# Moving four projection units behind the last turns of the feed-forward stages, and the last residual behind four rotary turns

## The chip, the cores and the metric

The kernel is one program on one core of a Trainium2 chip. The metric is the device time of an execution in microseconds; a measurement is the median of several runs. All matrix work is on TensorE (PE), element work on VectorE (DVE), ScalarE (ACT) and GpSimd (POOL), and SyncE (SP) issues the DMAs.

## The reference

Two pre-layernorm decoder layers on x (8 sequences of 112 tokens, width 512; 896 tokens, so seven tiles of 128). Each layer is self-attention, cross-attention and a feed-forward block:

```
x = x + L0_attn(layernorm(x));  x = x + L0_xattn(layernorm(x), ctx);  x = x + L0_ffn(layernorm(x))
x = x + L1_attn(layernorm(x));  x = x + L1_xattn(layernorm(x), ctx);  x = x + L1_ffn(layernorm(x))

L0_ffn: h = bitlinear(x, w_fc); h = gelu(h); return bitlinear(h, w_proj)
bitlinear(x, w): layer-norm x, round-trip it through absmax quantization, multiply by ternarized w
L1_attn: q = x @ Wq.T (16 heads of 128); k, v = x @ Wk.T, x @ Wv.T (4 heads)
         q, k = rope(q), rope(k); softmax(q k / sqrt(128), causal window) v; @ Wo.T
```

The change lies where L0_ffn ends and the query and key projections of L1_attn begin.

## The kernel before

The program is written as one queue of instructions for each engine, stage by stage, with semaphores between them. An engine works through its queue in the order written, so the order below is the order of the work. Products are made with operands split in two parts: XT[0] holds the rounded transposed activations and XT[1] the remainder; a weight piece lies in HL in the same two parts (round_w on ACT makes the first, rest_w on POOL the second). `mm3` (L250 to L252) issues three matmuls for one product.

**The feed-forward stages** (`pe_ffn`, `act_ffn`, `dve_ffn`, `pool_ffn`) run over st = 0 to 8. In stage st tile f = st goes through the first product (L1309, PSUM banks 0 to 3) and GELU, tile p = st - 2 is turned (four `turn`s of four transposes each, L255, banks 4 to 6), split in two parts by ACT and DVE (L1330, L1363) and multiplied by the second weights (`product`, L1294, 32 matmuls into bank 7), and the finished tile r = st - 3 is turned for the next layer. In stages 7 and 8 there is no first product any more, only p = 5, 6 and r = 4, 5.

`norm` on DVE follows the product of tile t: it adds to x (L1387), takes statistics (L1390, L1392), waits for ACT's root (L1358) and writes the normalised rows xn (L1398). `ln_turn` on PE (L322) waits for xn and transposes it into bank 7. `ln_hi` on ACT (L327) copies it rounded to XT[0], and `ln_lo` on DVE (L331) subtracts to get XT[1]. `product` of tile t waits for the ln_lo of tile t - 1, since they share bank 7.

**The projection** (`pe_proj1`, `dve_proj1`, `pool_proj1`) has 40 units, made by `unit1`. A unit is 12 matmuls, 128 columns of weight against half of the tokens (448), into bank u % 8. Units 0 to 3 are two weight pieces (q1, 0 and 1) against the first half of the tokens, which lie in tiles 0 to 3; unit 4 is the first that reads the second half, so it waits for ln_lo of tile 6. `unit1` waits for the multiplications of unit u - 8 before it writes its bank again. For each unit DVE makes three multiplications for the rotary embedding (L1498 to L1500), and POOL adds their results (L1511). DVE's unit u waits for POOL's unit u - 2, since there are two buffers rt. The V products follow on PE behind unit 39, then the attention. When POOL has summed the unit that ends a weight piece (the first time unit 5), it makes the second part of the piece three further on.

PE's order before, in stage 7: turn (5,0), turn (5,1), unit 0, ln_turn of tile 4, turn (5,2), turn (5,3), product of tile 5. In stage 8: the same with tile 6, unit 1 and ln_turn of tile 5. `pe_proj1` then has unit 2, ln_turn of tile 6, unit 3, the wait for ln_lo of tile 6, unit 4 and on. On DVE ln_lo of tile 6 is the first instruction of `dve_proj1`, ahead of the multiplications of unit 0.

Of the kernel before, what the change touches and what calls it, by code (L numbers as in the profile page):

```python
# [15 lines left out]
P, NT = 128, NB * S // 128  # L16
# [57 lines left out]
def build(nc, g):  # L74
# [8 lines left out]
    with ExitStack() as ctx:  # L83
# [136 lines left out]
        def done(sem, *point, by=1):  # L220
            count[sem] = count.get(sem, 0) + by
            assert live[0] or (sem, point) not in value, (sem, point)
            value[sem, point] = count[sem]
            return handle(sem), by
# [4 lines left out]
        def upon(sem, *point):  # L229
            return handle(sem), value[sem, point] if live[0] else 1  # L230
# [18 lines left out]
        def mm3(e, out, lh, ll, rh, rl, start, stop):  # L249
            e.matmul(out, lh, rh, start=start, stop=False)  # L250
            e.matmul(out, lh, rl, start=False, stop=False)  # L251
            return e.matmul(out, ll, rh, start=False, stop=stop)  # L252

        def tr(e, out, in_, n):
            return e.transpose(out, in_, C("ident", n)[:, 0:n])  # L255
# [6 lines left out]
        def k4(bank):  # L262
            return PS[:, bank, :].rearrange("p (k s) -> p k s", k=4)

        def XTt(hl, t):
            return XT[:, hl, :, t * P:(t + 1) * P]
# [8 lines left out]
        def slot(k):  # L275
            return HL[cut_no[k] % NHL]
# [22 lines left out]
        def has_w(e, k):  # L299
            e.wait_ge(*upon("pool_w", k))  # L300
            return slot(k)
# [19 lines left out]
        def ln_turn(e, tag, t, src, bank):  # L321
            e.wait_ge(*upon("dve_ln", tag, t, "xn"))  # L322
            turn4(e, src, bank).then_inc(*done("pe_ln", tag, t))
# [5 lines left out]
        def ln_lo(e, tag, t, bank):  # L329
            e.wait_ge(*upon("act_ln", tag, t, "hi"))  # L330
            e.tensor_tensor(XTt(1, t), k4(bank), XTt(0, t).bitcast(F), A.subtract).then_inc(*done("dve_ln", tag, t, "lo"))  # L331
# [761 lines left out]
        def w_rows(which, m, c):  # L1093
            return which[m][0][:, c, :] if m == 0 or c < 14 else which[m][1][:, c - 14, :]
# [87 lines left out]
        def quant_turn(e, t):  # L1182
            e.wait_ge(*upon("dve_fq", "y", t))
            if t < 4:
                e.wait_ge(*(upon("dve_fq", "lo", t - 1) if t else upon("dve_ox", "v", OX - 1)))
            turn4(e, xz[t % 4], q_bank(t)).then_inc(*done("pe_fq", t))
# [76 lines left out]
        def at_step(st):  # L1263
            return (st if st < NT else None, st - 2 if st >= 2 else None, st - 3 if st >= 3 else None)

        def g_of(t):
            return Gb[t % 3][:, :, :].rearrange("p a c -> p (a c)")


        def late_quant(st, n):  # L1270
            return {(0, 1): 4, (0, 3): 5, (1, 1): 6}.get((st, n))

        def pe_ffn(e):
            def turn(t, c4):
                if c4 == 0:
                    e.wait_ge(*upon("pool_f", "y", t))
                if c4 == 3:
                    e.wait_ge(*upon("dve_f", "lo", t, 0))
                elif t == 0:
                    e.wait_ge(*upon("dve_fq", "lo", 4 + c4))  # L1280
                else:
                    e.wait_ge(*upon("dve_f", "lo", t - 1, 3 if c4 == 0 else c4))
                for kc in range(4):
                    o = (c4 * 4 + kc) * 128
                    last = tr(e, PS[:, 4 + c4 % 3, kc * P:(kc + 1) * P], g_of(t)[:, o:o + 128], P)
                last.then_inc(*done("pe_f", "turn", t, c4))

            def product(t, c4):
                e.wait_ge(*upon("dve_f", "lo", t, c4))
                if c4 == 0:  # L1290
                    e.wait_ge(*(upon("dve_ln", "lnf", t - 1, "lo") if t else upon("act_sign", 1, 6)))
                for kc in range(4):
                    for hl in range(2):
                        last = e.matmul(PS[:, 7, :], YT[c4][:, hl, kc, :], w_rows(ter, 1, c4 * 4 + kc),  # L1294
                                        start=c4 == 0 and kc == 0 and hl == 0, stop=c4 == 3 and kc == 3 and hl == 1)
                last.then_inc(*done("pe_f", "pj", t, c4))

            e.wait_ge(*upon("act_sign", 0, 7))
            for st in range(NT + 2):
                f, p, r = at_step(st)  # L1300
                for n in range(4):
                    if f is not None:
                        if n == 0:
                            e.wait_ge(*upon("dve_fq", "lo", f))
                        if st:
                            e.wait_ge(*upon("act_f", "g", f - 1, n))
                        for kc in range(4):
                            for hl in range(2):
                                last = e.matmul(PS[:, n, :], XT[:, hl, kc, f * P:(f + 1) * P], w_rows(ter, 0, 4 * kc + n),  # L1309
                                                start=kc == 0 and hl == 0, stop=kc == 3 and hl == 1)  # L1310
                        last.then_inc(*done("pe_f", "fc", f, n))
                    if late_quant(st, n):
                        quant_turn(e, late_quant(st, n))
                    if p is not None and n != 2:
                        turn(p, min(n, 2))
                    if n == 2 and st >= NT:
                        unit1(e, st - NT)
                    if r is not None and n == 2:
                        ln_turn(e, "lnf", r, xn[r % 2], 7)
                if p is not None:  # L1320
                    turn(p, 3)
                    for c4 in range(4):
                        product(p, c4)

# [98 lines left out]
        def pool_ffn(e):  # L1423
            for t in range(NT):
# [8 lines left out]
        units1 = ([("q1", i, e_, h) for h in (0, 1) for i in range(2) for e_ in range(2)]  # L1433
                  + [(kind, i, e_, h) for kind, a, n in (("q1", 2, 8), ("k1", 0, 2)) for i in range(a, n)
                     for e_ in range(2) for h in range(2)])
# [11 lines left out]
        def unit1(e, u):  # L1447
            kind, i, e_, half = units1[u]
            k = piece[kind, i][0]
            if e_ == 0 and (u < 4 or u > 7 and half == 0):  # L1450
                has_w(e, k)
            if u == 0:
                e.wait_ge(*upon("act_f", "g", NT - 1, 3))
                e.wait_ge(*upon("dve_ln", "lnf", 3, "lo"))
            if u > 7:
                e.wait_ge(*upon("dve_p1", u - 8))
            project(e, slot(k), 128 * e_, half, u % 8).then_inc(*done("pe_p1", u))
            if u in ended1:
                freed[k] = "pe_p1", u

        def pe_proj1(e):
            for u in range(2, len(units1)):
                if u == 3:
                    ln_turn(e, "lnf", NT - 1, xn[0], 7)
                if u == 4:
                    e.wait_ge(*upon("dve_ln", "lnf", NT - 1, "lo"))
                unit1(e, u)
            for vh in range(2):
                k = piece["v1", vh][0]
                w = has_w(e, k)  # L1470
                for b in range(NB):
                    e.wait_ge(*(upon("act_v1", 0, b) if vh else upon("dve_p1", 32 + b)))
                    for kc in range(4):
                        o = kc * 256
                        last = mm3(e, PS[0:S, b, 0:256], XT[:, 0, kc, b * S:(b + 1) * S], XT[:, 1, kc, b * S:(b + 1) * S],
                                   w[:, 0, o:o + 256], w[:, 1, o:o + 256], kc == 0, kc == 3)
                    last.then_inc(*done("pe_v1", vh, b))
                freed[k] = "pe_v1", vh, 7
# [9 lines left out]
                round_w(e, piece["o1", 1 + vh][0])  # L1488

        def dve_proj1(e):  # L1490
            ln_lo(e, "lnf", NT - 1, 7)
            for u in range(len(units1)):
                u0, u1 = [rt[u % 2][:, j, :].rearrange("p (b s) -> p b s", b=4) for j in range(2)]
                bank = u % 8
                if u > 1:
                    e.wait_ge(*upon("pool_p1", u - 2))
                e.wait_ge(*upon("pe_p1", u))
                e.tensor_tensor(u0, psv(bank), b4(C("cos1")), A.mult)  # L1498
                e.tensor_tensor(u1[0:64], psv(bank, 64, 128), b4(C("sin1")[64:128]), A.mult)
                e.tensor_tensor(u1[64:128], psv(bank, 0, 64), b4(C("sin1")[0:64]), A.mult).then_inc(*done("dve_p1", u))  # L1500
# [976 lines left out]
```

## Time and profile before

| | |
|---|---|
| median of 3 runs | 1756.52 us (1754.92 to 1761.06) |
| the profiled execution, its own time | 1756.52 us |
| its span, first to last instruction | 1754.7 us |
| PE busy | 94% of the span |
| DVE busy | 58% |
| ACT busy | 41% |
| POOL busy | 28% |
| mean granted TensorE clock | 0.977 of full speed |

The profile is one execution seen by the hardware profiler. Each row of a timeline gives an instruction or a run of like ones: start and length in us, engine, line of the kernel, output and inputs, count, and in brackets how long the engine sat idle before it and what released it. Matmuls overlap in the array, so a matmul's length is longer than the distance to the next start; starts are the better ruler. PEclk is the granted clock as a share of full speed.

### The profile page before, as it was taken

The numbers are of one execution on the slowest core, as the hardware profiler recorded it, in microseconds if no ns is written. First come the engines' busy times: TensorE is split into PE (matmuls) and PEld (weight loads), VectorE is DVE, ScalarE is ACT, GpSimd is POOL, SyncE is SP. The second block draws the span as 40 slices with busy tenths as digits, with TensorE's granted clock in tenths as the row PEclk, the third lists the DMA queues.
The fourth block names the chain that finished last, engine by engine and source line by source line (L and its number), as shares of the span: only waits on it lengthen the run. The fifth ranks groups of instructions, "written<-read, shape, count | busy, mean of one in ns | idle before, by whom it ended". The sixth has DMA issues, their size and how long they took to land.

```text
span 1754.7 us, 24103 instructions
## 1 busy us (share of the span) xinstructions
PE 1642.1 (94%) x9652; PEld 1360.8 (78%) x9652; DVE 1020.4 (58%) x1719; ACT 726.4 (41%) x1220; POOL 497.6 (28%) x324
## 2 busy tenths in 40 slices
PE   5998999989899999989999989999788999989999
PEld 4997666868678888767889987777567788877887
DVE  5554564264557675577758757354756545554545
ACT  2111555222367775647521146222435334343332
POOL 2971443340100001321117734111512322212221
PEclk9998999989999999999999999999889999999999
DMA  3210002213321103410001110110001111111111
GB/s 133 72 49 14 2 1 80 83 49 114 105 89 52 34 1 138 153 49 1 1 1 61 48 37 1 47 36 30 19 1 54 37 55 49 61 43 36 55 61 42
DMA packets 28018, 87.48 MB, mean 50 GB/s; under 512 B 4090, under 2 KB 4090, under 8 KB 27655
## 3 DMA queue, kind: packets, MB, share of 16 engines
q1 hardware_dynamic: 27908, 85.94, 14.8%
q8 instruction: 77, 1.26, 0.3%
q14 instruction: 33, 0.27, 0.1%
HBM read 84.10 MB, written 1.84 MB: 49 GB/s over the span
## 4 chain that ended last, share of the span: by engine, by line
PE 80%; DVE 8%; ACT 7%; issue 2%; DMA 1%; POOL 1%; SPq 0%; ACTq 0%; DVEq 0%
PE PS L250 17%; PE PS L252 16%; PE PS L251 16%; PE PS L255 6%; PE PS L957 4%; PE PS L975 4%; PE PS L1294 3%; PE PS L845 3%; PE PS L1309 2%; PE PS L518 2%; ACT Sk L586 1%; PE PS L1543 1%; ACT PT L578 1%; PE PS L1531 1%; DMA stg<-in_wst 1%
## 5 line engine op out<-in xcount | busy, mean ns | idle before, releaser
L296 POOL TENSOR_TENSOR HL<-stg,HL 128x1024 fp32r<-128x1024 f32 (+2 forms) x109 | 237.9, 2185 | 866.2 <-ACT HL L291 866.2
L250 PE MATMUL PS<-XT,HL 128*128 128x448 f32 x608 | 224.8, 370 | 8.3 <-DVE XT L331 6.1
L251 PE MATMUL PS<-XT,HL 128*128 128x448 f32 x608 | 223.1, 367 | 0.0
L252 PE MATMUL PS<-XT,HL 128*128 128x448 f32 x608 | 223.1, 367 | 0.0
L291 ACT ACTIVATE HL<-stg 128x1024 fp32r<-128x1024 f32 (+2 forms) x109 | 102.2, 943 | 261.5 <-PE PS L252 240.8
L250 PE MATMUL PS<-HL,XT 128*128 128x512 f32 (+1 forms) x380 | 139.0, 366 | 8.9 <-DVE XT L678 7.4
L251 PE MATMUL PS<-HL,XT 128*128 128x512 f32 (+1 forms) x380 | 136.0, 358 | 0.0
L252 PE MATMUL PS<-HL,XT 128*128 128x512 f32 (+1 forms) x380 | 135.9, 358 | 0.0
L250 PEld LDWEIGHTS PS<-XT,HL 128*128 128x128 f32 x608 | 115.0, 189 | 19.7 <-DVE XT L331 5.3
L251 PEld LDWEIGHTS PS<-XT,HL 128*128 128x128 f32 x608 | 115.0, 189 | 9.2
L252 PEld LDWEIGHTS PS<-XT,HL 128*128 128x128 f32 x608 | 114.9, 189 | 9.1
L2112 DVE SCALAR_TENSOR_TENSOR Hh<-PS,sml,Hh 128x448 fp32r<-128x448 f32 x64 | 43.2, 682 | 106.7 <-ACT Hh L2006 106.5
L678 DVE TENSOR_TENSOR XT<-QO,XT 128x896 fp32r<-128x896 f32 x32 | 45.0, 1432 | 98.5 <-ACT XT L672 98.5
L957 PE MATMUL PS<-kvT,QO 128*112 128x375 f32 x256 | 92.5, 484 | 2.7 <-ACT Sx L1002 2.0
L250 PE MATMUL PS<-HL,Ph 128*128 128x512 f32 x224 | 91.2, 407 | 3.7 <-DVE ACC L2135 1.8
L1021 DVE TENSOR_REDUCE nm<-PS 112x2 f32<-112x750 f32 x64 | 60.1, 939 | 51.6 <-PE PS L957 51.6
L250 PEld LDWEIGHTS PS<-HL,XT 128*128 128x128 f32 (+1 forms) x380 | 70.9, 187 | 22.9 <-issue 7.0
L252 PE MATMUL PS<-HL,Ph 128*128 128x512 f32 x224 | 88.2, 394 | 0.0
L251 PE MATMUL PS<-HL,Ph 128*128 128x512 f32 x224 | 88.0, 393 | 0.0
L975 PE MATMUL PS<-PX,kvr 125*128 125x224 f32 x384 | 85.3, 359 | 0.0
L2006 ACT ACTIVATE Hh<-PS,sml 128x448 fp32r<-128x448 f32 x64 | 40.4, 634 | 103.0 <-PE PS L252 103.0
L651 POOL TENSOR_TENSOR Sk<-Sk,rc 112x896 f32<-112x896 f32 x32 | 53.3, 1682 | 100.2 <-DVE rc L633 100.2
(285 smaller groups left out, 3705.4 us busy)
## 6 DMA issues: line engine op xcount, KB each, us to landing
stg<-in_wst SPq DMA_DIRECT2D x85, 512.0 KB, 3.4
stg<-in_wst SPq DMA_DIRECT2D x16, 352.0 KB, 3.2
stg<-in_wst SPq DMA_DIRECT2D x16, 320.0 KB, 3.7
wsum<-in_wfc SPq DMA_DIRECT2D x8, 512.0 KB, 4.9
wsum<-in_wpj SPq DMA_DIRECT2D x8, 512.0 KB, 3.6
raw<-in_wfc SPq DMA_DIRECT2D x8, 512.0 KB, 7.6
stg<-in_wst SPq DMA_DIRECT2D x16, 256.0 KB, 2.6
raw<-in_wpj SPq DMA_DIRECT2D x7, 512.0 KB, 7.2
```

What stands on the lines that cost most here:

```text
L250: e.matmul(out, lh, rh, start=start, stop=False)
L251: e.matmul(out, lh, rl, start=False, stop=False)
L252: return e.matmul(out, ll, rh, start=False, stop=stop)
L255: return e.transpose(out, in_, C("ident", n)[:, 0:n])
L291: e.activation(slot(k)[:, 0, 0:n], stg[k % NSTG][:, 0:n], ACT.Copy).then_inc(*done("act_w", k))
L296: e.tensor_tensor(slot(k)[:, 1, 0:n], stg[k % NSTG][:, 0:n], slot(k)[:, 0, 0:n].bitcast(F), A.subtract).then_inc(*done("pool_w", k))
L651: e.tensor_tensor(p, p, b8(rc[:, k, :]), A.mult).then_inc(*done("pool_a0", "p", u))
L845: last = e.matmul(out, Mhl[i][:, a, kc, :], XT[:, c, kc, hs], start=kc == 0 and j == 0, stop=kc == 3 and j == 2)
L957: last = e.matmul(PS[0:S, bank + e_, 0:L], QO[:, 1 + st // 4, 2 * (st % 4) + e_, :], kvT[:, b, :], start=True, stop=True)
L975: last = e.matmul(PS[:, 6 + u % 2, 0:2 * S], kvr[:, c, u // 4 % 8, :], PX[u % 2][:, :, c, :], start=c == 0, stop=c == 2)
L1021: e.tensor_reduce(nm[:, st % 4, :], PS[0:S, bank:bank + 2, 0:L], AX.X, A.max, negate=True).then_inc(*done("dve_x", "nm", st))
L1294: last = e.matmul(PS[:, 7, :], YT[c4][:, hl, kc, :], w_rows(ter, 1, c4 * 4 + kc), start=c4 == 0 and kc == 0 and hl == 0, stop=c4 == 3 and ...
```

## The change

Units 0 and 1 go from the middle of stages 7 and 8 to behind the last turn of stage 7, ahead of the product of tile 5. Units 2 and 3 go from `pe_proj1` to the same place in stage 8, ahead of the product of tile 6. `pe_proj1` begins with ln_turn of tile 6 and the wait for its ln_lo, then unit 4. On DVE, ln_lo of tile 6 goes from ahead of the multiplications of unit 0 to ahead of those of unit 4, behind those of units 0 to 3. No arithmetic, buffer, DMA or semaphore is added or removed.

```diff
                     if p is not None and n != 2:
                         turn(p, min(n, 2))
-                    if n == 2 and st >= NT:
-                        unit1(e, st - NT)
                     if r is not None and n == 2:
                         ln_turn(e, "lnf", r, xn[r % 2], 7)
                 if p is not None:
                     turn(p, 3)
+                    if st >= NT:
+                        for u in range(2 * (st - NT), 2 * (st - NT) + 2):
+                            unit1(e, u)
                     for c4 in range(4):
                         product(p, c4)
...
         def pe_proj1(e):
-            for u in range(2, len(units1)):
-                if u == 3:
+            for u in range(4, len(units1)):
+                if u == 4:
                     ln_turn(e, "lnf", NT - 1, xn[0], 7)
-                if u == 4:
                     e.wait_ge(*upon("dve_ln", "lnf", NT - 1, "lo"))
                 unit1(e, u)
...
         def dve_proj1(e):
-            ln_lo(e, "lnf", NT - 1, 7)
             for u in range(len(units1)):
+                if u == 4:
+                    ln_lo(e, "lnf", NT - 1, 7)
```

## Rows read from the trace of the kernel before

**Rows 1.** The page: busy time by engine, and the chain that ended last.

```profile
PE 1642.1 (94%) x9652; PEld 1360.8 (78%) x9652; DVE 1020.4 (58%) x1719; ACT 726.4 (41%) x1220; POOL 497.6 (28%) x324
...
PE 80%; DVE 8%; ACT 7%; issue 2%; DMA 1%; POOL 1%; SPq 0%; ACTq 0%; DVEq 0%
```

**Rows 2.** Busy time by stretch, PE alone: us, busy (instructions), granted clock, DMA share, GB/s.

```profile
885.00:917.00 32.00, 30.13 (x159) 1.00 0.00 1
916.67:1026.90 110.23, 110.23 (x625) 1.00 0.16 53
```

**Rows 3.** Timeline of PE in stage 7: start, length in us; idle before, and releaser.

```profile
885.01 1.04 PE L255 MATMUL PS<-cst,Gb 128*128 128x128 f32 x8
885.80 0.45 PE L250 MATMUL PS<-XT,HL 128*128 128x448 f32 x1
...
888.32 0.60 PE L255 MATMUL PS<-cst,xn 128*128 128x128 f32 x4
888.75 1.04 PE L255 MATMUL PS<-cst,Gb 128*128 128x128 f32 x8
890.42 0.94 PE L1294 MATMUL PS<-ter,YT 128*128 128x512 f32 x3 [0.63 <-DVE XT L331]
```

**Rows 4.** Timeline of PE from stage 8's product on, and the first V product.

```profile
903.21 6.60 PE L1294 MATMUL PS<-ter,YT 128*128 128x512 f32 x28 [0.63 <-DVE XT L331]
909.64 1.07 PE L1294 MATMUL PS<-ter1e,YT 128*128 128x512 f32 x4
...
913.75 0.66 PE L255 MATMUL PS<-cst,xn 128*128 128x128 f32 x4 [0.61 <-DVE xn L1398]
...
916.67 0.36 PE L250 MATMUL PS<-XT,HL 128*128 128x448 f32 x1
...
1004.22 0.28 PE L250 MATMUL PS<-HL,XT 128*112 128x256 f32 x1
```

**Rows 5.** Timeline of DVE, stages 7 and 8 and behind them.

```profile
887.61 0.55 DVE L1398 TENSOR_SCALAR xn<-x,mvl,rsl 128x512 f32<-128x512 f32 x1
888.07 1.28 DVE L1363 TENSOR_TENSOR YT<-PS,YT 128x512 fp32r<-128x512 f32 x2
889.58 0.69 DVE L331 TENSOR_TENSOR XT<-PS,XT 128x512 fp32r<-128x512 f32 x1 [0.23 <-ACT XT L327]
...
913.15 0.55 DVE L1398 TENSOR_SCALAR xn<-x,mvl,rsl 128x512 f32<-128x512 f32 x1
915.07 0.69 DVE L331 TENSOR_TENSOR XT<-PS,XT 128x512 fp32r<-128x512 f32 x1 [1.38 <-ACT XT L327]
915.68 0.61 DVE L1498 TENSOR_TENSOR rt<-PS,cst 128x448 f32<-128x448 f32 x1
...
917.60 0.62 DVE L1498 TENSOR_TENSOR rt<-PS,cst 128x448 f32<-128x448 f32 x1
```

**Rows 6.** Timeline of POOL: unit 0's sum, and the first weight piece behind the change.

```profile
917.65 1.16 POOL L1511 TENSOR_TENSOR QO<-rt 128x448 f32<-128x448 f32 x1 [30.70 <-DVE rt L1500]
...
928.39 2.40 POOL L296 TENSOR_TENSOR HL<-stg,HL 128x1024 fp32r<-128x1024 f32 x1
```

**Rows 7.** Waits of PE from 916 to 1040 us: total, times, longest.

```profile
PE PS L255 <- POOL Sb L1572: 1.2, 1, 1.2
```

**Rows 8.** Windows around holes of PE: columns as in rows 2.

```profile
742.00:748.00 6.00, 3.85 (x16) 1.00 0.25 81
766.00:778.00 12.00, 9.70 (x41) 0.86 0.00 0
804.00:814.00 10.00, 7.96 (x32) 0.83 0.01 2
1159.00:1172.00 13.00, 8.95 (x32) 0.87 0.11 40
481.00:492.00 11.00, 7.24 (x24) 0.69 0.55 194
372.00:400.00 28.00, 20.73 (x97) 0.70 0.32 102
```

## The prediction

> **What bounds the kernel now.** I read the page first: TensorE (PE) is busy for 94% of the span, and the chain that ended last lies on it for 80% [rows 1]. So a change costs or gains what it does to the holes in PE's stream. Next, busy time by stretch. Around the moved units, from 885 us to the start of unit 4 (916.67), PE is busy for 30.13 of 32.00 us: it has 1.87 us of holes there, which is all that a new order could win. From unit 4 to the end of the V products PE is busy for 110.23 of 110.23 us [rows 2]: whatever delays unit 4 delays the whole rest. The reader is to see that the first number bounds the gain, and that the second takes away any later repayment.
>
> Then the timelines of PE and VectorE (DVE). Three things fill the time of a norm. In stage 7, two turns start at 885.01, unit 0 runs from 885.80 to the turn of the normalised rows at 888.32, and those rows are finished by DVE at 887.61 + 0.55 = 888.16 [rows 3, 5]. The unit therefore hides the norm, to within 0.2 us. Stage 8 is the same 12.79 us later (product at 903.21 against 890.42), with unit 1 [rows 3, 4]. Behind the last product, unit 2 hides most of the third norm (0.61 us left), and unit 3 hides the copy and the subtraction L331 [rows 4, 5].
>
> **The change part by part.**
>
> *Units 0 and 1 leave the hole of the norm.* Unit 0 no longer stands between the turns and ln_turn of tile 4, and unit 1 is no longer in stage 8. In stage 7, PE ends the two turns at 885.01 + 1.04 = 886.05, and has nothing to do until the rows at 888.16; the first transpose after such a wait comes 0.05 us later (913.15 + 0.55 = 913.70, then 913.75), so at 888.21: a new hole of 2.16 us [rows 3 to 5]. ln_turn starts only 0.11 us earlier than before. Its four transposes take 0.43 us to the next start and eight turns 0.79 us [rows 3], so the units can start at 888.21 + 0.43 + 0.79 = 889.43. The last turn needs the first split of tile 5, which DVE makes first in the pair at 888.07 (1.28 us for two), so by about 888.7; no wait [rows 5].
>
> *Two units per stage behind the turns.* A unit that follows transposes takes 888.32 - 885.80 = 2.52 us, one that follows a unit 2.43 us: units 4 to 39, 36 of them, take from 916.67 to the first V product at 1004.22 [rows 3, 4]. 889.43 + 2.52 + 2.43 = 894.38 for the start of the product, against 890.42: **+3.96 us**. The hole of 0.63 us ahead of the product goes, since splits and L331 are done by then; it is in this difference already. Stage 8 is the same pattern with units 2 and 3: again +3.96 us, together **+7.92 us**. Of that 4.86 us is work brought forward from behind the last product.
>
> *Behind the last product nothing is left to hide the norm of tile 6.* The last product ends at 909.64 + 1.07 = 910.71 in the trace of before, and the rows are ready at 913.70 [rows 4, 5]. All 2.99 us of it is idle now.
>
> *DVE turns four units before it does L331.* This is the costly edit. The DVE queue is written out in order. Before, L331 of tile 6 (dve_proj1's ln_lo) ran at 915.07 and the rotary multiplications of unit 0 came behind it at 915.68. Now the multiplications of units 0 to 3 stand first. None of them waits: their products are long there, and GpSimd's sum, which a unit's multiplications wait for two units later, takes 1.16 us [rows 6] of a unit's 1.92 us. Their period is 917.60 - 915.68 = 1.92 us, so four take 7.69 us [rows 5]. They start as the norm ends, 0.08 us before its modelled end as the split at 888.07 does against 888.16, so at 913.62. L331 starts at 921.31 and ends at 922.00. PE starts 0.15 us behind such an end (889.58 + 0.69 = 890.27 against 890.42 in the stage before; I take this lag for unit 4 too). Unit 4 starts at 922.15, that is 11.44 us behind the last product. Queued behind L331 on DVE are the multiplications of unit 4 on, which need PE's unit 4 anyway; PE's whole queue waits for L331. ScalarE's copy of tile 6 is ready long before, as it was at 915.07.
>
> Before, unit 4 started 916.67 - 910.71 = 5.96 us behind the product, with two units in that time [rows 4]. So this end costs 11.44 - 5.96 = **+5.48 us**. Sum on PE at an unchanged clock: 7.92 + 5.48 = **+13.4 us**.
>
> *What it doesn't cost.* The bytes, weights and matmuls are the same, and no DMA is moved in its queue. The first new weight piece is finished by GpSimd at 928.39 + 2.40, behind its sum of unit 5 [rows 6], for unit 12. GpSimd is four units ahead in the new order when unit 4 starts, so it is earlier against PE than now, when PE doesn't wait. That cover is PE's own 19 us from unit 4 to unit 12 (eight units of 2.43 us); without it a late piece costs what it is late by. The head start of DVE and GpSimd is worth nothing: in the stretch to 1040 PE's longest wait is for GpSimd in the attention, 1.2 us [rows 7], and in the 110 us of units and V products there is none [rows 2].
>
> *TensorE's clock.* A hole can cost more than its length. The windows around holes of before show it [rows 8], each around one long hole but for the last row: idle time is the window less PE's busy time, and time lost to the clock is window x (1 - PEclk), as the granted clock has two levels, 1.2 and 2.4 GHz. Around 804 to 814 (2.04 us idle) 10 x 0.17 = 1.7 us is lost; at 766 (2.30 us idle) 12 x 0.14 = 1.7; at 1159 (4.05 idle) 13 x 0.13 = 1.7; at 481 (3.76 idle) 11 x 0.31 = 3.4. But 742 to 748 (2.15 idle) lost nothing. The new holes are 2.16 us in stages 7 and 8, and behind the last product 2.99 us plus, behind one turn (913.75 + 0.66 = 914.41), 922.15 - 914.41 = 7.74 us, more than any of these. For the last I take one fall, **1.7 us** (ends: 0 and 3.4, taken from the rows at 1159 and 481; nearer 1159, since units of long matmuls follow it). For each short hole I take 0.6 as the chance of a fall (two of the three rows nearest in length fell). One fall of the two is likelier (0.48) than both (0.36) or none (0.16): **1.7 us**, ends 0 and 3.4.
>
> The Trainium skill (TensorE: Matmul & The Clock Gate, HAM oscillation) warns only of holes longer than these two short ones. By it the short ones lose nothing, and the sum would be 15.1 us in place of 16.8. The hole in the window from 804, as short, did lose 1.7 us in this trace, so I go by the row and keep the rule as a rival.
>
> **Sum.** 13.4 + 1.7 + 1.7 = +16.8 us. The profiled execution took 1756.52 us for a span of 1754.7, and is itself the median of the three runs (1754.92 to 1761.06). 1756.5 + 16.8 = **1773.3 us**, slower by 0.96%. No change is anything within 0.3%, 5.3 us.
>
> **The rivals.**
> - *Both short holes lower the clock:* 13.4 + 1.7 + 3.4 = 18.5, 1775.0 us. The rows at 766 and 804 speak for it, 742 against.
> - *Only the long hole does:* 15.1, 1771.6 us. Beside it: this is what the page of the Trainium skill named above would lead to. The row at 804 speaks against.
> - *The clock stays up everywhere:* 13.4, 1769.9 us. Against it: both windows with over 3.5 us idle lost some, and 7.7 us is far more.
> - *The clock costs more:* behind the long hole 3.4 or, as at 372 to 400 [rows 8], where PE had hole after hole, 28 x 0.30 = 8.4 us. With one short hole that is 18.5 to 23.5 us, 1775 to 1780. Against it: unit 4 on is a stream without holes, and 372 to 400 was none.
> - *Not slower:* the three holes of before (0.63, 0.63, 0.61 us) go and no new one comes, which gives 1756.5 - 1.9 = 1754.6 us. The place is L331 of tile 6: it decides if DVE has done the four units' multiplications before PE is through its last product. But DVE's norm of tile 6 needs that product and stands ahead of them in the queue. A gain beyond 0.3% isn't to be had at all, as the stretch has only 1.87 us of holes [rows 2].
>
> **How the numbers follow.** The three ways the short holes can go, 0.48, 0.36 and 0.16, share the 0.83 that the other cases leave: forecast 0.40; both short holes 0.30; only the long one 0.13; clock unchanged 0.05; clock costs more 0.09; not slower 0.03. The range takes 1769.9 (less 1.6, the lowest of the runs before against their median) and 1775.0 plus 3, into the dearer case and the runs' upward spread: 1768.3 to 1778. All but the last case are over 0.3% slower: slower 0.96, same 0.03, faster 0.01.
>
> **What would show it.** In stages 7 and 8: a hole of 2.2 us ahead of ln_turn that waits for xn L1398, then two units in a row, and no wait for L331 at the product; product starts 16.75 us apart, or up to 1.7 more. Behind the last product: about 3.0 us idle, one turn, then 7.7 us idle, ended by L331, which starts right behind twelve multiplications of DVE. From there to the attention a PE as full as now, with a stretch at half the clock first. The prediction is wrong if L331 comes ahead of the multiplications, if PE waits for weights in unit 12, or if PE falls behind DVE's head start and wins something back in the attention.

## The result and the profile after

The changed kernel is slower: ratio 1.0069 to the kernel before, 95% interval 1.0044 to 1.0095, medians 1771.4 us (1762.67 to 1773.69) and 1756.45 us, six runs each. By the ratio that is +12.2 us, by the medians +15.0. A second comparison, in experiment 5, gave 1.0088 (1.0063 to 1.0113). The profiled execution took 1766.8 us with a span of 1765.0 us, against 1756.52 and 1754.7; it lies 4.6 us below the changed kernel's median.

The timeline of PE of the changed kernel, stage 7 to unit 4, and the first V product, answers to [rows 3] and [rows 4]:

```profile
885.23 1.04 PE L255 MATMUL PS<-cst,Gb 128*128 128x128 f32 x8
888.43 0.66 PE L255 MATMUL PS<-cst,xn 128*128 128x128 f32 x4 [2.16 <-DVE xn L1399]
888.93 1.04 PE L255 MATMUL PS<-cst,Gb 128*128 128x128 f32 x8
889.72 0.45 PE L250 MATMUL PS<-XT,HL 128*128 128x448 f32 x1
...
894.66 6.52 PE L1294 MATMUL PS<-ter,YT 128*128 128x512 f32 x28
...
911.35 6.52 PE L1294 MATMUL PS<-ter,YT 128*128 128x512 f32 x28
917.71 1.07 PE L1294 MATMUL PS<-ter1e,YT 128*128 128x512 f32 x4
921.81 1.11 PE L255 MATMUL PS<-cst,xn 128*128 128x128 f32 x4 [3.03 <-DVE xn L1399]
930.12 0.74 PE L250 MATMUL PS<-XT,HL 128*128 128x448 f32 x1 [7.19 <-DVE XT L331]
...
1019.89 0.28 PE L250 MATMUL PS<-HL,XT 128*112 128x256 f32 x1
```

The brackets are what to read. Four waits stand where before there were three of 0.6 us: 2.16 us for the normalised rows in stage 7 (and again in stage 8), 3.03 us for those of tile 6, and 7.19 us for L331. The product of tile 6 starts 16.69 us behind that of tile 5, where it was 12.79.

The timeline of DVE says why the last one is so long; it answers to the lower half of [rows 5]. (The change adds one line ahead of these, so L1398 and L1498 of before are L1399 and L1499 here.)

```profile
921.21 0.55 DVE L1399 TENSOR_SCALAR xn<-x,mvl,rsl 128x512 f32<-128x512 f32 x1
921.67 0.62 DVE L1499 TENSOR_TENSOR rt<-PS,cst 128x448 f32<-128x448 f32 x1
...
923.59 0.62 DVE L1499 TENSOR_TENSOR rt<-PS,cst 128x448 f32<-128x448 f32 x1
...
927.44 0.62 DVE L1499 TENSOR_TENSOR rt<-PS,cst 128x448 f32<-128x448 f32 x1
...
929.37 0.69 DVE L331 TENSOR_TENSOR XT<-PS,XT 128x512 fp32r<-128x512 f32 x1
```

L331 carries no bracket: DVE was not idle before it. It went from the norm straight into the multiplications of units 0 to 3, 1.92 us each, and PE waited for the last instruction behind them.

The windows of PE (us, busy, granted clock, DMA share, GB/s) answer to [rows 2] and [rows 8]:

```profile
880.00:900.00 20.00, 17.84 (x92) 1.00 0.00 1
900.00:915.00 15.00, 12.84 (x71) 1.00 0.00 1
918.80:921.10 2.30, 0.00 (x0) 1.00 0.00 0
921.10:930.00 8.90, 1.11 (x4) 0.50 0.00 0
930.00:934.80 4.80, 4.68 (x13) 0.50 0.00 0
934.80:940.00 5.20, 5.20 (x27) 1.00 0.01 2
940.00:1020.00 80.00, 80.00 (x397) 1.00 0.18 60
...
1149.89:1219.89 70.00, 64.56 (x293) 0.98 0.14 46
1219.89:1329.89 110.00, 89.56 (x884) 0.94 0.03 11
```

The two short holes left the clock alone. Behind the last product it fell at 921.10, 2.3 us into the wait of 3.03 us and ahead of the one of 7.19; it stayed down through that one and the first 4.8 us of units. From 940 on PE is full. The last two rows are of work much later, 130 to 310 us behind the first V product, and matter below.

**A ruler for the stretch.** The times of one kernel scatter by some 11 us here (by 18 us, 1762.38 to 1780.34, over all 23 runs on record of the changed kernel), so I measure each trace from the first turn of stage 7 to the first V product. Before that is 1004.22 - 885.01 = 119.21 us [rows 3, 4]. It has three parts: to the end of the last product (25.70), from there to unit 4 (5.96), and units 4 to 39 (87.55). The first two are the order of the work, the third tells the clock, and the pace from one matmul's start to the next. In the changed kernel they are 33.55, 11.34 and 89.77 us, together 134.66: **+15.45 us**, of which the order is 7.85 + 5.38 = +13.23 and the units +2.22.

### The profile page after: what moved, and what is told of

The parts are those of the page before. It is cut to its first block, busy times and chain, and to the rows that moved or that the text cites. A ratio compares the mean times of both kernels' runs of the same rounds, so it can differ in the third digit from the quotient of the medians.

```text
span 1765.0 us, 24103 instructions
## 1 busy us (share of the span) xinstructions
PE 1640.7 (93%) x9652; PEld 1360.0 (77%) x9652; DVE 1020.3 (58%) x1719; ACT 726.9 (41%) x1220; POOL 497.2 (28%) x324
## 3 DMA queue, kind: packets, MB, share of 16 engines
HBM read 84.10 MB, written 1.84 MB: 49 GB/s over the span
## 4 chain that ended last, share of the span: by engine, by line
PE 80%; DVE 9%; ACT 7%; issue 2%; DMA 1%; POOL 1%; SPq 0%; ACTq 0%; DVEq 0%
PE PS L250 17%; PE PS L252 16%; PE PS L251 16%; PE PS L255 6%; PE PS L975 4%; PE PS L957 4%; PE PS L1294 3%; PE PS L845 3%; PE PS L1309 2%; PE PS L518 2%; ACT Sk L586 1%; PE PS L1544 1%; ACT PT L578 1%; PE PS L1532 1%; DMA stg<-in_wst 1%
## 5 line engine op out<-in xcount | busy, mean ns | idle before, releaser
L250 PE MATMUL PS<-HL,XT 128*128 128x512 f32 (+1 forms) x380 | 137.1, 361 | 8.8 <-DVE XT L678 7.4
L251 PE MATMUL PS<-HL,XT 128*128 128x512 f32 (+1 forms) x380 | 134.7, 355 | 0.0
L252 PE MATMUL PS<-HL,XT 128*128 128x512 f32 (+1 forms) x380 | 134.7, 354 | 0.0
```

## The experiments

**1. VectorE's order undone.**

```diff
         def dve_proj1(e):
+            ln_lo(e, "lnf", NT - 1, 7)
             for u in range(len(units1)):
-                if u == 4:
-                    ln_lo(e, "lnf", NT - 1, 7)
```

> The changed kernel with ln_lo of tile 6 back ahead of the multiplications of unit 0 on VectorE; all four units still lie behind the turns. My theory (VectorE's order delays unit 4; the units' place costs the rest): unit 4 starts 5.2 to 5.7 us behind the last product, not 11.4; product starts stay 16.7 us apart; 7.2 us slower than before plus 0 to 3.4 us of lowered clock, so 0.4 to 0.6%. Rival (the whole loss is the units taken out of the holes of the norm, VectorE's order is hidden): time as the changed kernel, 12 to 15 us slower than before.

Ratio 1.0054 (1.0041 to 1.0067), some 9.5 us. The timeline of PE in this kernel:

```profile
912.41 1.07 PE L1294 MATMUL PS<-ter1e,YT 128*128 128x512 f32 x4
916.51 1.11 PE L255 MATMUL PS<-cst,xn 128*128 128x128 f32 x4 [3.03 <-DVE xn L1399]
919.04 0.74 PE L250 MATMUL PS<-XT,HL 128*128 128x448 f32 x1 [1.41 <-DVE XT L331]
```

The wait for L331 falls from 7.19 to 1.41 us and unit 4 starts 5.56 us behind the product. The stages stay as in the changed kernel (33.56 us). The order costs 7.86 - 0.40 = +7.46 us: VectorE's place for one instruction was 5.8 us of the loss. The rival, that VectorE's order is hidden, falls by the trace; the times alone don't settle it, as the interval overlaps the changed kernel's. The clock fell here too, 2.7 us into the wait of 3.03 us (1.00 from 913.50 to 916.20, then 0.50 to 923): the fall doesn't need the long wait for L331. Units 4 to 39 took 91.17 us, 3.62 more than before, by the clock and the pace of experiment 5.

**2. VectorE's order alone,** in the kernel before: L331 behind four units' multiplications, TensorE's queue untouched.

```diff
         def dve_proj1(e):
-            ln_lo(e, "lnf", NT - 1, 7)
             for u in range(len(units1)):
+                if u == 4:
+                    ln_lo(e, "lnf", NT - 1, 7)
```

> The kernel before with only VectorE's order changed: ln_lo of tile 6 behind the multiplications of units 0 to 3; TensorE's order as before. My theory: unit 4 starts 11.4 us behind the last product in place of 5.96, a hole of 5.5 us, so +5.5 us plus 1.7 to 2.4 us of lowered clock: 0.4 to 0.45% slower than before; product starts stay 12.8 us apart. Rival (hidden behind units 2 and 3): within 0.5 us of before.

Ratio 1.0049 (1.0037 to 1.0061), some 8.6 us. PE of this kernel:

```profile
906.68 1.07 PE L1294 MATMUL PS<-ter1e,YT 128*128 128x512 f32 x4
910.78 0.66 PE L255 MATMUL PS<-cst,xn 128*128 128x128 f32 x4 [0.60 <-DVE xn L1398]
...
919.09 0.74 PE L250 MATMUL PS<-XT,HL 128*128 128x448 f32 x1 [5.22 <-DVE XT L331]
```

Units 2 and 3 hide a part of the wait and no more, and the rival "hidden" falls by the trace and by the time: 919.09 - 907.75 = 11.34 us from product to unit 4, exactly as in the changed kernel, +5.38 us. Stages are as before (25.73 us). The units lose 2.71 us to the clock, which here fell in the hole of 5.22 us.

**3. One unit kept in the hole, one moved,** L331 first.

```diff
+                    if n == 2 and st >= NT:
+                        unit1(e, 2 * (st - NT))
                     if r is not None and n == 2:
                         ln_turn(e, "lnf", r, xn[r % 2], 7)
                 if p is not None:
                     turn(p, 3)
                     if st >= NT:
-                        for u in range(2 * (st - NT), 2 * (st - NT) + 2):
-                            unit1(e, u)
+                        unit1(e, 2 * (st - NT) + 1)
...
         def dve_proj1(e):
+            ln_lo(e, "lnf", NT - 1, 7)
             for u in range(len(units1)):
-                if u == 4:
-                    ln_lo(e, "lnf", NT - 1, 7)
```

> One unit stays in the hole of the norm in stages 7 and 8 (0, then 2), one goes behind the last turn (1, then 3), and ln_lo of tile 6 is first on VectorE. My theory: moving units forward costs only where it opens a hole, so each stage grows by one unit less the old wait of 0.63 us (product starts about 14.5 us apart) and unit 4 starts 5.2 us behind the last product: 2 x 1.7 + 5.2 - 5.96 = +2.6 us over before, up to 1.7 us more if the clock falls, 0.15 to 0.25%. Rival (two units ahead of the product are dear wherever they stand, since they delay norm by their whole length): as e1, 0.4% or more.

Ratio 1.0026 (1.0011 to 1.0041). PE of this kernel:

```profile
885.18 0.60 PE L255 MATMUL PS<-cst,xn 128*128 128x128 f32 x4
...
888.92 6.53 PE L1294 MATMUL PS<-ter,YT 128*128 128x512 f32 x28
...
903.26 6.54 PE L1294 MATMUL PS<-ter,YT 128*128 128x512 f32 x28
909.63 1.07 PE L1294 MATMUL PS<-ter1e,YT 128*128 128x512 f32 x4
...
915.80 0.74 PE L250 MATMUL PS<-XT,HL 128*128 128x448 f32 x1 [1.41 <-DVE XT L331]
```

No bracket stands ahead of ln_turn or of the products: the holes of 2.16 and of 0.63 us in the stages are gone, products start 14.34 us apart, and two units' work (4.86 us) went forward for 3.13 us. Unit 4 starts 915.80 - 910.70 = 5.10 us behind the product, 0.86 less than before. The order costs 3.13 - 0.86 = +2.27 us, against +7.46 with the holes left open. (The units took 92.04 us in this trace, 4.49 more than before: the clock behind the wait of 3.03 us, and the pace of experiment 5.) In this order what a unit costs depends on whether it leaves a hole behind, not on its lying ahead of the product; the +2.27 us that are left go with the waits behind the last product (3.03 and 1.41 us in place of 0.61), where no unit stands any more.

**4. Half the dose:** in the changed kernel, `if u == 4` of `dve_proj1` becomes `if u == 2`.

> The changed kernel with ln_lo of tile 6 behind two units' multiplications on VectorE instead of four. My theory: half of the dose, 2 x 1.92 = 3.84 us less than the changed kernel: unit 4 starts 7.6 us behind the last product, and the kernel is 9.5 us slower than before plus 1.7 to 2.4 us of clock, 0.6 to 0.7%. Rival (what counts is whether ln_lo is first or not, or the hole's clock alone): time as e1 or as the changed kernel.

Ratio 1.006 (1.0048 to 1.0072). PE of this kernel:

```profile
917.19 1.07 PE L1294 MATMUL PS<-ter1e,YT 128*128 128x512 f32 x4
921.29 1.11 PE L255 MATMUL PS<-cst,xn 128*128 128x128 f32 x4 [3.03 <-DVE xn L1399]
925.74 0.74 PE L250 MATMUL PS<-XT,HL 128*128 128x448 f32 x1 [3.34 <-DVE XT L331]
```

Unit 4 starts 7.48 us behind the product. This, too, is a reading of the trace: the times don't tell the kernel from experiment 1 or from the changed kernel. From four units to two the wait falls by 11.34 - 7.48 = 3.86 us, 1.93 us for each unit. From two to none it falls by 1.92 in all, since then the way over PE's turn and ScalarE's copy ends last: in experiment 1 VectorE is idle for 1.84 us ahead of L331, released by ScalarE's L327.

**5. The changed kernel again,** unedited.

> The changed kernel as it is, on the chip of the next three, for comparison with them and for a second profile. My theory: the order of work is the same (product starts 16.7 us apart, unit 4 11.4 us behind the last product, unit stream begun at half the clock), 0.6 to 1.0% slower than before; the short holes may or may not lower the clock this time. Rival (the difference to before comes from the state of the chip): the second ratio lies well away from 1.007.

Ratio 1.0088 (1.0063 to 1.0113), median 1770.56 us. The order is the same to 0.01 us (33.55 and 11.33). But units 4 to 39 took 1020.68 - 929.15 = 91.53 us in place of 89.77. The group view of both traces from 940 to 1000 us, at full clock in both, shows where. First profile, then this one:

```profile
L251 PE MATMUL PS<-XT,HL 128*128 128x448 f32 x99 | 36.2, 365 | 0.0
```

```profile
L251 PE MATMUL PS<-XT,HL 128*128 128x448 f32 x98 | 36.1, 368 | 0.0
```

A matmul is 368 ns long in place of 365. From start to start it is 206.7 ns in place of 202.7 (mean of over 370 distances), 1.7 us over the 432 matmuls of the 36 units. Nothing of the program differs. The rival, a state of the chip that makes the difference to before, doesn't show: the second ratio lies within the first one's interval.

**6. TensorE kept at work behind the last product.** The changed kernel with 48 matmuls more, whose result nobody reads, 12 in the wait of 3.03 us and 36 in that of 7.19.

```diff
                 if u == 4:
+                    project(e, slot(piece["q1", 0][0]), 0, 0, 6)
                     ln_turn(e, "lnf", NT - 1, xn[0], 7)
+                    for _ in range(3):
+                        project(e, slot(piece["q1", 0][0]), 0, 0, 6)
                     e.wait_ge(*upon("dve_ln", "lnf", NT - 1, "lo"))
```

> The changed kernel with TensorE kept at work behind the last product: one unit's twelve matmuls on the first weight piece ahead of ln_turn of tile 6 and three times twelve behind it, into bank 6, which unit 6 overwrites. It adds 48 matmuls whose result nobody reads. My theory (1.7 to 2.4 us of the loss are the clock that fell in the long hole): the added work fits in the idle time (2.43 of 2.99 us, 7.3 of 7.6 us), unit 4 still starts 11.4 us behind the product but at the full clock: 2 to 3.5 us (0.1 to 0.2%) faster than the changed kernel. Rival (the hole costs its length and no more): as the changed kernel or slower by what the added work overruns.

Ratio 1.0093 (1.0065 to 1.012): the gain of 2 to 3.5 us that I expected isn't there in the times. The windows of PE:

```profile
915.00:926.00 11.00, 10.39 (x52) 1.00 0.00 0
926.00:940.00 14.00, 13.64 (x67) 1.00 0.00 1
1148.83:1218.83 70.00, 64.67 (x289) 0.95 0.14 45
1218.83:1328.83 110.00, 89.50 (x863) 0.88 0.03 11
```

The clock stays up, unit 4 starts 11.34 us behind the product, but the units ran at the slower pace (89.38 us). The whole stretch is 134.27 us, 2.1 us less than in the trace of experiment 5, which had the same pace. The last two rows show why it doesn't come out in the time of this execution. 130 to 310 us behind the first V product, where nothing is changed, the clock was granted 0.95 and 0.88 here and 0.98 and 0.94 in the first profile of the changed kernel. From the V product to the end this trace takes 752.8 us, the other 745.1. Whether the added matmuls have a part in that, one profile can't show.

**7. All new holes filled:** as 6, and in stages 7 and 8, ahead of ln_turn, nine matmuls that nobody reads, into bank 3.

```diff
+                        if st >= NT:
...
+                            w = slot(piece["q1", 0][0])
+                            for kc in range(3):
+                                mm3(e, PS[:, 3, 0:HT], w[:, 0, kc * 256:kc * 256 + 128], w[:, 1, kc * 256:kc * 256 + 128],
+                                    XT[:, 0, kc, 0:HT], XT[:, 1, kc, 0:HT], kc == 0, kc == 2)
                         ln_turn(e, "lnf", r, xn[r % 2], 7)
```

> As the busy wait, and nine more matmuls nobody reads in each of the two holes of 2.16 us ahead of ln_turn in stages 7 and 8 (1.9 us, into bank 3). My theory: no fall of the clock between 880 us and the attention in any run, so the loss to before is the order alone, +13.4 us (0.76%), and against the changed kernel 2 to 4 us less on average. Rival (the clock isn't moved by holes of 2 us in this place): as the busy wait.

Ratio 1.0086 (1.0055 to 1.0118), again not told apart from the changed kernel by time, where I expected 2 to 4 us less. Here is the cleanest trace, though:

```profile
884.00:900.00 16.00, 15.65 (x83) 1.00 0.00 1
900.00:915.00 15.00, 14.65 (x75) 1.00 0.00 1
915.00:926.00 11.00, 10.39 (x54) 1.00 0.00 0
926.00:940.00 14.00, 13.65 (x68) 1.00 0.10 35
```

```profile
881.89 1.04 PE L255 MATMUL PS<-cst,Gb 128*128 128x128 f32 x8
...
926.81 0.47 PE L250 MATMUL PS<-XT,HL 128*128 128x448 f32 x1 [0.35 <-DVE XT L331]
...
1014.47 0.28 PE L250 MATMUL PS<-HL,XT 128*112 128x256 f32 x1
```

Full clock, fast pace, and the stretch is 1014.47 - 881.89 = 132.58 us: **+13.37 us** over before. That is the price of the order by itself. But the rival of this experiment holds: in experiment 6 the two holes of 2.16 us stood open and the clock was at 1.00 behind them as well, so filling them gained nothing.

**8. The small waits of before removed another way.** The kernel before, with the normalised rows of tiles 4 and 5 turned into banks that are free, so that the product need not wait for L331.

```diff
-                        ln_turn(e, "lnf", r, xn[r % 2], 7)
+                        ln_turn(e, "lnf", r, xn[r % 2], r - 2 if st >= NT else 7)
...
-                if c4 == 0:
+                if c4 == 0 and t >= NT - 2:
+                    e.wait_ge(*upon("dve_f", "x", t - 1))
+                elif c4 == 0:
...
+            if u in (2, 3):
+                e.wait_ge(*upon("dve_ln", "lnf", u + 2, "lo"))
```

(ln_hi and ln_lo read the same bank.)

> Not the change but the kernel before, with the waits of 0.63 us taken away in another way: ln_turn of tiles 4 and 5 goes into banks 2 and 3, which are free in stages 7 and 8, so the product in bank 7 need not wait for L331. My theory: the two holes of 0.63 us go, product starts come 12.2 us apart, and the kernel is 1.2 us faster than before (0.07%), which the trace shows and the times can't. Rival (the product then waits for the splits of its own tile instead): starts stay 12.8 us apart.

Ratio 0.9996 (0.9974 to 1.0019). PE of this kernel:

```profile
887.37 6.64 PE L1296 MATMUL PS<-ter,YT 128*128 128x512 f32 x28
...
899.29 6.62 PE L1296 MATMUL PS<-ter,YT 128*128 128x512 f32 x28
```

Products start 11.92 us apart in place of 12.79, and the stretch is 1.73 us shorter than before. That is more than the two waits of 0.63 us: a product that follows the turns without a wait also starts 0.2 us sooner. As expected, the times can't show it: the version is better by its trace and not by its measurement.

## Why the prediction was right or wrong

The sign, the range and the mechanism of the order were right; of the two terms of the clock one was wrong and one too small. Forecast was 1773.3 us, +16.8; measured, by the ratios, +12.2 us (0.69% of 1756.5) and, the second time, +15.4 us (0.88% of 1753.2), by the medians +15.0 and +17.3. That the median of 1771.4 lies 1.9 us from the forecast is partly luck, as the part of the program that nothing touches scatters by 8 us and one term of 1.7 us didn't come. By its own steps:

- *Two units per stage, +7.92 us.* Shown: 33.55 - 25.70 = +7.85. The new hole was forecast at 2.16 us and is 2.16 us in the trace, both times. The start of the product was forecast 9.37 us behind the first turn and is 9.43.
- *The norm of tile 6 bare, 2.99 us:* 3.03.
- *L331 behind four units, unit 4 at 11.44 us, +5.48:* 11.34, +5.38. Experiment 1 undoes this term, 2 has it alone, and 4 has half of it, at 1.93 us for each unit.
- *Sum at an unchanged clock, +13.4:* 13.23 in the changed kernel, and 13.37 in experiment 7, which holds clock and pace still.
- *The clock behind the long hole, 1.7 us:* mis-sized. Units 4 to 39 took 2.22 us more. In the other kernels with a hole there, at the fast pace, it was 2.71 (experiment 2) and 2.42 us (experiment 4), all within the ends that I took, 0 and 3.4. I had put it down to the hole of 7.7 us; in the traces the clock fell already in the wait of 3.03 us ahead of it, and in experiment 1 with no long wait at all.
- *The clock in the short holes, 1.7 us:* wrong. This term was the difference of the forecast from its rival "only the long hole does", and the rival's 15.1 us is the better: the stretch grew by 15.45. These two holes stood open in five profiles (the first of the changed kernel and experiments 1, 4, 5 and 6), ten holes in all, and the clock fell in none. The Trainium skill (TensorE: Matmul & The Clock Gate, HAM oscillation) was right for these holes, where I had gone by rows of other places. It isn't right everywhere, as the last section shows. One of my rows was also misread: the window from 742 to 748 ends inside the next hole, and of its 2.15 us idle 1.97 are the hole that I meant. So the chance of 0.6 rested on three rows that don't tell much of these two places.
- *Nothing given back later:* PE is full from 940 to 1020 us, as forecast, and no wait for weights appears. Yet the span grew by only 10.3 us, as the rest behind the first V product took 745.1 us, and 750.5 before. No instruction of it is changed. In ten traces this rest takes 744.9 to 752.8 us and goes with the clock: over the same 180 us of it, window x (1 - PEclk) is 8.0 us where it takes 745.1, 13.5 at 750.5 and 16.7 at 752.8. Whether the delay itself moves these falls is open: the three shortest rests are the changed kernel's two (745.1, 746.7) and experiment 4's (744.9), and the other seven take 749.3 or more. So the span of a single profile says little about a sum of 13 us, and the stretch says much.
- *The rival "not slower"* asked for the multiplications to be done ahead of the last product's end. DVE's queue doesn't let them, and the trace shows them behind the norm.

Not foreseen at all: the pace of 206.7 ns, 1.7 us in some executions.

## What to carry to other kernels

Before moving independent work out of the middle of a stage, ask what it covers there: a unit of 2.4 us stood in a hole of 2.2 us. Moved behind the next twelve matmuls, all of them turns, it hid nothing there, and the hole stayed open. In a queue that runs in order, the instruction that releases the bottleneck engine goes ahead of any work whose result is not yet wanted: one subtraction of 0.69 us, put behind 7.7 us of such work, cost 5.4 us. When runs scatter by as much as the effect, measure the stretch between two landmarks of the traces, and keep the clock apart from the order.

## What the runs showed of the hardware that was not expected

*Length alone doesn't tell whether a hole lowers the clock.* The windows of the changed kernel at the places of [rows 8], and around the hole of 1.82 us at 1376:

```profile
742.00:748.00 6.00, 4.03 (x17) 0.92 0.26 79
766.00:778.00 12.00, 9.13 (x46) 1.00 0.00 0
804.00:814.00 10.00, 7.99 (x32) 0.83 0.01 2
1374.00:1384.00 10.00, 8.18 (x30) 0.83 0.06 13
```

Against [rows 8], the holes of 1.97 us (near 744) and 2.30 us (near 769) have changed roles. Over the ten traces the clock was below full behind the hole of 1.82 us in all, of 2.03 us (near 806) in all, of 1.97 us in nine (ahead of the hole of 3.35 us that follows it), of 2.30 us in two, and behind the new ones of 2.16 us in none. The place counts, it seems, and not alone, since one place gives both outcomes; what else does stays open.

*A stream of like matmuls has two paces.* At full clock and without a wait, units 4 to 39 ran at 202.7 ns from start to start in six of the ten traces and at 206.7 ns in four (experiments 1, 3, 5 and 6), from the stream's start to its end. One of the four is the changed kernel itself, which had the other pace in its first profile. The pace belongs to a stream and not to an execution: in experiment 1 units 0 to 3, at 886 to 890 us, still ran at 202.7. And in experiment 8 the projection of the first layer had the slow pace (first row, 80 to 120 us) and that of the second the fast one (second row, 940 to 998 us):

```profile
L250 PE MATMUL PS<-XT,HL 128*128 128x448 f32 x65 | 23.9, 368 | 0.0
L251 PE MATMUL PS<-XT,HL 128*128 128x448 f32 x96 | 35.1, 365 | 0.0
```

It goes with neither the order, nor a lowered clock ahead of the stream: experiment 6 had none and was slow. The cause wasn't found.
